# A residual network block on one core: another order of the work ahead of the convolution taps

## Time and profile before

| | us |
|---|---|
| median of 3 runs | 248.98 |
| lowest and highest | 248.55, 249.33 |
| profiled execution, its own time | 249.21 |
| span in its profile | 247.4 |
| TensorE busy | 202.0 (82%) |
| VectorE busy | 141.8 (57%) |
| ScalarE busy | 131.2 (53%) |
| GpSimd busy | 91.2 (37%) |

### The profile page before, as it was taken

The page is one execution under the profiler, slowest core; times in us unless marked ns, Lnnn a source line. Parts: engine busy times, 40 slices in busy tenths (PEclk is TensorE's granted clock), DMA queues, the critical chain, the costliest instruction groups (busy, mean ns, idle before and its releaser), DMA issues.

```text
span 247.4 us, 3489 instructions
## 1 busy us (share of the span) xinstructions
PE 202.0 (82%) x1126; PEld 73.7 (30%) x1126; DVE 141.8 (57%) x351; ACT 131.2 (53%) x222; POOL 91.2 (37%) x202
## 2 busy tenths in 40 slices
PE   0002997899999999999999996999999789996133
PEld 0001232354233232332342331234333124333132
DVE  0598866724156664466766676155685624559931
ACT  0477689933218659277566578118558630941400
POOL 1004042146234231341755841163674205063830
PEclk9999999799999999999999999579999956999855
DMA  6999999955597999689999999996999999411595
GB/s 239 413 408 411 407 409 410 299 148 115 140 206 148 242 216 236 128 213 248 213 232 275 264 282 247 233 212 150 249 278 269 271 239 206 169 53 35 180 378 205
DMA packets 30802, 59.85 MB, mean 242 GB/s; under 512 B 3264, under 2 KB 12224, under 8 KB 30784
## 3 DMA queue, kind: packets, MB, share of 16 engines
q1 hardware_dynamic: 30400, 59.34, 83.3%
q10 hardware_dynamic: 384, 0.29, 0.4%
HBM read 17.85 MB, written 16.78 MB: 140 GB/s over the span
## 4 chain that ended last, share of the span: by engine, by line
PE 71%; DMA 8%; SPq 7%; DVE 6%; POOL 4%; issue 3%; POOLq 0%; DVEq 0%
PE py L769 37%; PE pf L799 23%; DMA xs<-x_dram 8%; SPq L248 7%; PE py L715 4%; PE pf L715 3%; PE py L814 3%; POOL xs L240 1%; DVE xs L610 1%; DVE gs L518 1%; DVE blk L627 1%; POOL gs L327 1%; PE py L806 1%; POOL chain L365 1%; DVE b L636 0%
## 5 line engine op out<-in xcount | busy, mean ns | idle before, releaser
L769 PE MATMUL py<-gs,wd 80*32 80x512 f32 x768 | 91.7, 624 | 5.1 <-issue 4.7
L489 ACT ACTIVATE junk<-xs,nwb 128x1024 bf16<-128x1024 f32 x60 | 68.9, 1148 | 8.2 <-DVE xs L610 5.9
L799 PE MATMUL pf<-y,fw 128*128 128x512 f32 x128 | 63.3, 640 | 1.2 <-DVE y L619 1.2
L610 DVE SCALAR_TENSOR_TENSOR xs<-pf,cst,xs 128x512 f32<-128x512 f32 x64 | 47.8, 750 | 23.2 <-PE pf L799 18.7
L352 POOL TENSOR_TENSOR wd<-vals,cst 80x384 f32<-80x384 f32 x30 | 25.3, 844 | 81.9 <-PE py L769 81.8
L470 ACT ACTIVATE y<-py,cst 128x512 f32<-128x512 f32 x32 | 20.2, 683 | 65.6 <-PE pf L799 63.1
L619 DVE SCALAR_TENSOR_TENSOR y<-py,cst,y 128x512 f32<-128x512 f32 x32 | 22.6, 746 | 38.6 <-PE py L769 38.6
L769 PEld LDWEIGHTS py<-gs,wd 80*32 80x32 f32 x768 | 23.9, 112 | 68.3 <-issue 68.1
L799 PEld LDWEIGHTS pf<-y,fw 128*128 128x128 f32 x128 | 24.7, 203 | 34.5 <-issue 33.2
L518 DVE BATCH_NORM_STATS2 gs<-xs 128x6 f32<-128x512 f32 x40 | 24.9, 680 | 14.3 <-DMA xs<-x_dram 14.1
L417 ACT ACTIVATE wd<-xs 128x1024 bf16<-128x1024 f32 x24 | 25.0, 1044 | 4.5 <-DMA xs<-x_dram 4.5
(11 more groups left out here) (77 smaller groups left out, 95.0 us busy)
## 6 DMA issues: line engine op xcount, KB each, us to landing
gs<-fc SPq DMA_DIRECT2D x128, 190.6 KB, 4.0
xs<-x_dram SPq DMA_DIRECT2D x15, 1024.0 KB, 18.6
out_dram<-xs SPq DMA_DIRECT2D x32, 256.0 KB, 4.0
out_dram<-xs SPq DMA_DIRECT2D x16, 512.0 KB, 4.6
xs<-x_dram SPq DMA_DIRECT2D x2, 512.0 KB, 17.6
gs<-wkv_dram SPq DMA_DIRECT2D x1, 256.0 KB, 15.6
gs<-wout_t_dram SPq DMA_DIRECT2D x1, 256.0 KB, 15.7
fw<-fusion_dram SPq DMA_DIRECT2D x1, 256.0 KB, 10.8
```

Of the source, the lines that this page charges most:

```text
L489: act.activation(junk[:, :], x1(n, c), func, scale=scale, bias=bias[:, c:c + 1], accum_out=acc[:, n, c, e:e + 1]).then_inc(s_stat, 1)
L610: dve.scalar_tensor_tensor(out=rows[:, t], in0=image(pf[:, bank * HALF:(bank + 1) * HALF]), scalar=fb[:, c:c + 1], in1=rows[:, t], op0=ALU ...
L769: mm = pe.matmul(py[n % 2][quad(q), s * HALF:(s + 1) * HALF], wd[0:KP, w0:w0 + QUAD], rows, start=(j == 0), stop=(j == PASSES - 1))
L799: pe.matmul(pf[:, bank * HALF:(bank + 1) * HALF], fw[:, t * C + 128 * c:t * C + 128 * (c + 1)], y[:, t * HALF:(t + 1) * HALF], start=True, ...
```

## The change

Four edits, all in the order of the work; no semaphore is added and the waits of the DMA queue stay as they are.

- VectorE: `variance(k-1)` comes before batch k's first sums. In the last batch VectorE takes channel half 1 of images 13, 14 and 15, and ScalarE half 0 of them (before: VectorE both halves of 14, ScalarE both of 13). `squares` works on two slices there.
- TensorE: three f images of batch 2 ahead of `groups(3)`, not two. `shifts(3)` behind the copy product. The second product of the attention matrix, which signals `s_atm`, goes behind the first taps and the bias product. ScalarE's copy of the matrix follows.
- VectorE: the weights of the first half image alone are added up and written first, then those of the second.
- ScalarE: some stores of f come earlier or later among the sums.

```diff
@@ ScalarE @@
             f_bias(0)
-            store_f(0, 0)
-            store_f(0, 1)
+            for j in range(3):
+                store_f(0, j)
             x_sums(9)
+            store_f(0, 3)
             x_sum(11, 0)
-            store_f(0, 2)
-            store_f(0, 3)
             f_bias(1)
             store_f(1, 0)
             store_f(1, 1)
-            x_sums(13)
+            x_sum(13, 0)
             store_f(1, 2)
+            x_sum(14, 0)
             x_sum(15, 0)
             store_f(1, 3)
             f_bias(2)
             for j in range(BATCH):
                 store_f(2, j)
-            act.wait_ge(s_atm, 1)
-            act.activation(at[:, :], pf[:, HW:HW + NC2 * C], ACT.Copy).then_inc(s_at, 1)
             f_bias(BATCHES - 1)
...
                 store_first(n)
                 if n == 0:
+                    act.wait_ge(s_atm, 1)
+                    act.activation(at[:, :], pf[:, HW:HW + NC2 * C], ACT.Copy).then_inc(s_at, 1)
                     late_f(0)
@@ VectorE @@
             for k in range(BATCHES):
-                x_stats(BATCH * k, (0, 1))
                 if k:
                     variance(k - 1)
-                x_stats(BATCH * k + 2, (0, 1))
+                x_stats(BATCH * k, (0, 1))
+                if k == BATCHES - 1:
+                    x_stats(N - 3, (1,))
                 if k:
                     pixel_means(k - 1)
+                x_stats(BATCH * k + 2, (0, 1) if k < BATCHES - 1 else (1,))
                 squares(k)
                 x_stats(BATCH * k + 3, (1,))
                 last_square(k)
...
+            dve.reduce_sum(gsum[0:KP, :], gr[0:KP, :].rearrange("p (g n) -> p g n", g=NG), AX.X)
             dve.tensor_tensor(vs[:, 0], table(awq, 0), g_of(0, 0), ALU.mult)
-            link(dve.reduce_sum(gsum[0:KP, :], gr[0:KP, :].rearrange("p (g n) -> p g n", g=NG), AX.X))
-            dve.tensor_tensor(vs[:, 1], table(awq, 1), g_of(0, 1), ALU.mult)
-            for s in range(2):
-                ins = dve.tensor_tensor(ds[:, s], table(cwq, s), per_group(gsum[0:KP, 4 * s:4 * s + 4]), ALU.mult)
-            link(ins)
+            link(dve.tensor_tensor(vs[:, 1], table(awq, 1), g_of(0, 1), ALU.mult))
+            dve.tensor_tensor(ds[:, 0], table(cwq, 0), per_group(gsum[0:KP, 0:4]), ALU.mult)
+            link(dve.tensor_tensor(vs[:, 0], vs[:, 0], table(dtq, 0), ALU.add))
+            link(dve.tensor_tensor(vs[:, 0], vs[:, 0], ds[:, 0], ALU.add))
+            for j0, j1 in ((0, 1), (1, PASSES)):
+                dve.scalar_tensor_tensor(out=diagonals(0, j0, j1), in0=spread(v0, 0, j0, j1), scalar=0.0,
+                                         in1=eyes(j0, j1), op0=ALU.max, op1=ALU.mult).then_inc(s_wd0, 1)
+            link(dve.tensor_tensor(ds[:, 1], table(cwq, 1), per_group(gsum[0:KP, 4:8]), ALU.mult))
...
@@ TensorE @@
             f_early(2, 1)
+            f_early(2, 2)
             groups(3)
-            f_early(2, 2)
             f_early(2, 3)
...
             mm.then_inc(s_gmm, 1)
-            shifts(3)
             pe.wait_ge(s_gx, 1)
             pe.matmul(pf[0:KP, GREP:GREP + NG * N], sel, gx[0:CM], start=True, stop=True).then_inc(s_rep, 1)
+            shifts(3)
             pe.wait_ge(s_attw, 32)
             attention_matrix(0)
-            attention_matrix(1).then_inc(s_atm, 1)
...
                     mm.then_inc(s_ybias, 1)
+                    attention_matrix(1).then_inc(s_atm, 1)
                     f_late(0)
```

More of the change, by code:

```diff
@@ L524, in squares @@
             def squares(k):
[L525 to L528, removed]
+                if k < BATCHES - 1:
+                    parts_ = ((mv[:, BATCH * k:BATCH * k + 3:2, :, :], 0, 4),)
+                else:
+                    parts_ = ((mv[:, BATCH * k:BATCH * k + 1, :, :], 0, 2), (mv[:, BATCH * k + 1:BATCH * k + 3, 1:2, :], 2, 4))
+                for m, a, b in parts_:
+                    s = sq[:, 4 * k + a:4 * k + b].rearrange("p (j c) -> p j c", c=m.shape[2])
+                    ins = dve.tensor_tensor(s, m[:, :, :, 0], m[:, :, :, 0], ALU.mult)
+                link(ins)
+                for m, a, b in parts_:
+                    s = sq[:, 4 * k + a:4 * k + b].rearrange("p (j c) -> p j c", c=m.shape[2])
+                    dve.tensor_tensor(m[:, :, :, 1], m[:, :, :, 1], s, ALU.add)
             def last_square(k):
@@ L598, in _ @@
             dve.wait_ge(s_gall, 1)
[L599 to L602, removed]
+            link(dve.tensor_tensor(vs[:, 1], vs[:, 1], ds[:, 1], ALU.add))
+            dve.scalar_tensor_tensor(out=diagonals(1, 0, PASSES), in0=spread(v0, 1, 0, PASSES), scalar=0.0,
+                                     in1=eyes(0, PASSES), op0=ALU.max, op1=ALU.mult).then_inc(s_wd0, 1)
             def residual(n):
```

## The result

The changed kernel is slower: median 254.68 us (252.54 to 257.01), before 248.76 (248.10 to 249.33), ratio 1.021 [1.014, 1.028]. The forecast was 252.0 with a range from 249.5 to 253.4: the direction and the place of the queue's wait were right, the size was not. Ratios leave out runs more than 1.5% above the fastest of the same kernel; medians are those of all runs. The profiled execution took 254.2 for a span of 252.4, which is 5.0 above the profiled one of before. Its mean granted clock was 0.910; the other three had 0.898 to 0.908, so they spent no less time at 1.2 GHz. Where they did is not on record.

The account below looks back on a forecast made before the run. TensorE, almost unbroken from the first tap, was taken as the bound (71% of the chain). Profiled 249.21 - 1.75 (front) + 3.3 (copies' wait) + 1.5 (clock) = 252.3, less 0.2 to the median: 252.0 us, range 249.5 to 253.4.

Parts of the forecast that it names:

- Front: Work before the first tap: earlier variance, split last batch and shorter weights chain start the taps 1.75 us earlier.
- the floor I had given (47.7): Earliest start of groups(3), in us; forecast 49.4 with a low clock stretch before it.
- T: Start of the first tap, 57.37 us before; forecast 55.6, bounds 3.4 earlier and 0.3 later.
- rival (a): Clock falls at only one idle: in front alone 250.6, before fuse(0) alone (second case) 250.8; chance 0.30.
- the likeliest case: Clock falls both in front and before fuse(0): 252.0 us, own range 251.3 to 252.9, chance 0.44.
- Attention product: Second attention product, moved behind the first taps, ends 4.25 us after the first tap and frees image 1's copies.
- Queue wait: DMA queue: image 1's copies issue later, delaying ScalarE's stores; fuse(0) 3.3 us later against the first tap.
- Clock at the new stall: TensorE's 2.25 us stall before fuse(0) brings the low clock, costing 1.5 us; bounds 0 and 4.5.
- Sum: Whole kernel: 249.21 - 1.75 + 3.3 + 1.5 = 252.3, less 0.2 to the median: 252.0 us.
- rival (c): Stalls at 152.09 and near 196 shift, and one no longer lowers the clock: 247.5 us; chance 0.09.
- Rival (d): Image 1's copies each land 2.7 us after issue, no clock fall before fuse(0): 249.0 us; chance 0.03.
- rival (b): Clock holds both in front and before fuse(0): 249.3 us, about no change; chance 0.09.

Follow-up runs that it names:

- Experiments 6 and 7: Changed kernel with three small unread dense matmuls before the first taps: 252.05 us (6); also with attention operands in tiles of their own: 247.97 us (7).
- experiment 1: Changed kernel with seven unread dense matmuls of 512 columns in TensorE's idle ahead of the first taps: median 254.2 us, ratio 1.017.
- experiment 9: Changed kernel with the second attention product back before the taps and two unread dense matmuls ahead of groups(2): median 246.28 us.
- experiments 5 and 10: Changed kernel, second attention product back before the taps: 245.11 us (5); plus unread dense matmuls before groups(2) and the taps of images 10 and 14: 241.05 us (10).
- experiment 4: Kernel before with only the second attention product and ScalarE's copy of the matrix moved behind the first taps: median 252.2 us.

## Why the prediction was wrong

- **Front.** Groups(3) was forecast at 49.4, with a fall of the clock before it. The profiled run had none there and 47.83, the floor I had given (47.7). Experiments 6 and 7 had it, at 49.43 and 49.49. T: 3.3 earlier against 1.75, inside my bounds. The idle before groups(2) was 2.59, and no fall followed, though one followed the 2.02 before fuse(0); so my premise that every idle over 1.5 brings one was wrong. Up to T the profiled execution went as the second case of rival (a), whose sum was 250.8. The miss of the likeliest case looks small only because its front was 1.5 too late. From groups(3) to T I had 6.23; it is 6.27. VectorE's shorter chain: 1.46 forecast, 1.47 measured (52.20 to 53.67).
- **Attention product: the step that failed.** "Now the product ends at T + 2.7 (taps) + 0.53 (bias product) + 1.0 = T + 4.25" took the full clock for granted. It ended at T + 8.2, since the clock was at 1.2 GHz from 53.3 to 63.6. I had costed what the moved product adds behind T and whom it holds, but put the clock at T at nothing. I looked only at idles in one piece, not at the light matmuls with idles of 0.62 and 0.44 that the shorter front leaves between 50.3 and 52.6. In experiment 1 dense work stands there and the product ends at T + 4.3. The fall was not set off by the missing product: it came while the first one ran, and experiment 9 had one with both in place. Why experiments 5 and 10 had none over the same matmuls stays open.
- **Queue wait.** First issue to freed ScalarE: 9.9 forecast, 10.04 measured. Fuse(0) against T: 3.3 later forecast, 7.6 in the changed kernel, of which 3.95 is the step above; in experiment 4, without it, 3.8.
- **Clock at the new stall.** Forecast 1.5, measured 1.64 (5.34 against 3.70), after an idle of 2.02.
- **Sum.** At the end of fuse(0) the forecast was -1.75 + 3.3 + 1.5 = 3.05 late; the trace has 79.11 against 73.12, so 6.0 = -3.3 + 7.6 + 1.6 and rounding. At the end it is 5.0, because a low stretch behind the wait at 158 lasted 6.8 us, not 10.2 as at 152 before. That is rival (c) in part, worth 1.4. The later wait for copies, near 200, then took 2.81 instead of 2.32.
```profile
158.08 2.46 issue
160.53 3.42 PE py L780 x24
...
164.50 6.01 PE pf L810 x8
```
- **Rival (d) and the skill.** By an estimate from the Trainium skill, "DMA: Bandwidth & Descriptors", section "Anatomy of one DMA — SWDGE (gpsimd) path", the eighth copy would have landed 2.4 us after its issue. The section gives its fit for DMAs issued by GpSimd, which I had left out; these are issued by SyncE. The rows decide: ScalarE was freed 10.0 after the first issue, not 7.9. The Trainium skill, "TensorE: Matmul & The Clock Gate", section "Why this matters for your kernels", warns only of idle gaps above some 3 us. By that the clock would have held at the new stall of 2.02. It fell in the changed kernel, and in experiments 4 and 1 after 2.52 and 2.93, so the rule is not safe here. At the idle of 2.59 in front it agrees with the trace. I had also applied the rule to one place only: by it the front would have kept the clock too, and the sum would have been the 249.3 of rival (b), not 250.6.
- The range was too narrow because both clock terms were bounded for one place each, and none for the first taps.

What stays open: why the clock falls in front or ahead of T in one execution and not in another over the same matmuls, and by how much each share counts in the median. I have one trace for each kernel.

## What to carry to other kernels

For an instruction that is moved, list three things: what it delays where it goes, who waits for its semaphore, directly or through a reused buffer and an in-order queue, and what it leaves behind where it was. On TensorE the last counts as well: a front that gets shorter can leave a stretch of light matmuls in which the clock falls, and what stands behind the stretch may decide how long it stays low (3.4 us with 2 us of dense products there, 10.2 with half of them; one and two profiles). If a kernel's runs spread by 1 to 2%, read the granted clock of each run before you read a gain into an order.

## What the hardware showed that I had not expected

- No long idle is needed for a fall: idles of 0.62 and 0.44 us between small matmuls came ahead of 1.2 GHz at 53.3, and 10.2 us passed before 2.4 GHz was back. The same matmuls did not bring it in every profile.
- Apart from the last one, which lasts to the end, the low stretches of all twelve profiles have three lengths: 3.4, 6.8 and 10.2 us.
- Work whose result nobody reads can pay: 2 x 1.98 us of it in two waits, with 1.98 in the front, took the median from 245.1 to 241.1. The two in the waits alone, in one set of runs, took it from 246.28 to 241.05.
- A 128x128 matmul of 512 float32 columns is two instructions, 0.94 us together; the f products with 64 columns of weights come to half for an instruction, 3.65 for 16.
